# Order of TensorE's work in a slot of a Mamba-2 mixer kernel: the state matmuls from the second place to the third

## What is computed

```python
h = rmsnorm(x) * norm_w
proj = einsum('bsd,od->bso', h, in_proj_w)     # gate 8192 | hidden 8192, B 1024, C 1024 | dt 128
hBC = silu(causal_conv(hBC, conv_w, conv_b))   # 4 taps
hid, B, C = split(hBC)                         # 128 heads of 64; 8 groups of B and C, 128 states each
dt = softplus(dt + dt_bias); A = -exp(A_log) * dt
# chunked scan, in effect: y[i] = sum_{j<=i} (C_i . B_j) exp(cs_i - cs_j) dt_j hid_j
y = (Y_diag + Y_off) + Dp * hid
yg = y * silu(gate)
y = yg * rsqrt(mean over the group's 1024 channels of yg^2 + eps) * gnorm_w
out = x + einsum('bsd,od->bso', y, out_proj_w)
```

## Time and profile before

| what | value |
|---|---|
| median of 3 runs | 846.28 us (846.05 to 847.78) |
| profiled execution: its time, and its span | 846.1 us, 844.4 us |
| mean granted TensorE clock | 0.984 |
| TensorE matmuls busy | 792.3 us (94%) |
| TensorE weight loads busy | 611.8 us (72%) |
| VectorE, ScalarE, POOL busy | 626.7 us (74%), 599.9 us (71%), 633.9 us (75%) |
| DMA | 94.93 MB, mean 112 GB/s |

### The profile page before, as it was taken

One profiled execution on the slowest core, in us unless ns is written; L12 is line 12 of the kernel. 1 busy time (PEld: TensorE's weight loads), 2 busy tenths in 40 slices (PEclk: granted clock), 3 DMA queues, 4 the chain that ended last, 5 costly groups with the idle time before them and its releaser, 6 DMA issues.

```text
span 844.4 us, 13293 instructions
## 1 busy us (share of the span) xinstructions
PE 792.3 (94%) x4313; PEld 611.8 (72%) x4316; DVE 626.7 (74%) x757; ACT 599.9 (71%) x1046; POOL 633.9 (75%) x568
## 2 busy tenths in 40 slices
PE   4788899999999999999999999999999999989686
PEld 3566677777777777777777778777777777767563
DVE  5858878868686876776786867787677778697773
ACT  2487777888778876888688877887788857875341
POOL 5497975789767986789578985798678967893450
PEclk9899999999999999999999999999999999999996
DMA  8253232433253324334233415333342424420001
GB/s 278 67 186 122 90 125 89 126 126 125 68 181 125 118 94 150 125 113 136 87 125 125 125 62 165 124 113 121 129 128 98 153 88 141 125 88 1 5 2 50
DMA packets 48812, 94.93 MB, mean 112 GB/s; under 512 B 3952, under 2 KB 36848, under 8 KB 48784
## 3 DMA queue, kind: packets, MB, share of 16 engines
q1 hardware_dynamic: 48784, 94.58, 34.2%
HBM read 93.26 MB, written 1.31 MB: 112 GB/s over the span
## 4 chain that ended last, share of the span: by engine, by line
PE 59%; DVE 19%; ACT 10%; issue 9%; POOL 1%; POOLq 1%; ACTq 0%; DVEq 0%
PE ps_z L1071 19%; PE ps_out L1177 15%; PE ps_h L1071 12%; PE ps_y L1164 7%; DVE conv_bc L729 4%; ACT decay L539 3%; DVE conv L729 3%; PE ps_t L1049 2%; DVE decay L787 2%; ACT L539 2%; ACT conv L487 2%; DVE v L842 2%; DVE yg L848 1%; ACT conv_bc L471 1%; DVE y_lo L854 1%
## 5 line engine op out<-in xcount | busy, mean ns | idle before, releaser
L729 DVE SCALAR_TENSOR_TENSOR conv<-ps_h,w_raw,conv 128x510 f32<-128x510 f32 (+2 forms) x192 | 143.3, 746 | 100.7 <-ACT conv L487 96.0
L539 ACT ACTIVATE decay<-csx,cs_own 128x256 f32<-128x256 f32 (+1 forms) x512 | 184.4, 443 | 1.2 <-POOL csx L342 0.2
L304 POOL TENSOR_TENSOR win_lo<-w_raw,win_hi 128x1024 fp32r<-128x1024 f32 x64 | 152.8, 2387 | 0.7 <-DMA csx<-cs_rows 0.7
L399 POOL TENSOR_TENSOR sqacc<-sqacc,sq 128x512 f32<-128x512 f32 x47 | 70.5, 1500 | 106.9 <-ACT sq L575 106.9
L787 DVE TENSOR_TENSOR decay<-decay,cbm 128x1536 f32<-128x1536 f32 x64 | 127.9, 1998 | 2.8 <-ACT decay L539 2.8
L547 ACT ACTIVATE hidT<-conv 128x512 f32<-128x512 f32 x64 | 40.5, 633 | 100.5 <-DVE conv L729 100.5
L1164 PE MATMUL ps_y<-decay,hid_dt 128*64 128x256 f32 (+1 forms) x1024 | 98.5, 335 | 13.7 <-DVE hid_dt L831 13.7
L1164 PEld LDWEIGHTS ps_y<-decay,hid_dt 128*64 128x64 f32 x1024 | 64.0, 137 | 56.4 <-DVE hid_dt L831 19.5
L342 POOL TENSOR_SCALAR_AFFINE_SELECT csx<-csx 128x512 f32<-128x512 f32 x128 | 104.1, 838 | 0.0
L1177 PE MATMUL ps_out<-wout_hi,y_lo 128*128 128x512 f32 x256 | 101.5, 396 | 0.0
L1177 PE MATMUL ps_out<-wout_hi,y_hi 128*128 128x512 f32 x256 | 101.1, 395 | 0.0
(11 more groups left out here) (300 smaller groups left out, 1500.3 us busy)
## 6 DMA issues: line engine op xcount, KB each, us to landing
w_raw<-in_wmain SPq DMA_DIRECT2D x64, 772.0 KB, 4.3
csx<-cs_rows SPq DMA_DIRECT2D x128, 256.0 KB, 3.5
bc_raw<-in_wbc SPq DMA_DIRECT2D x8, 517.0 KB, 3.5
ctx_raw<-in_ctx SPq DMA_DIRECT2D x1, 2048.0 KB, 12.8
acc<-in_x SPq DMA_DIRECT2D x4, 256.0 KB, 3.4
bc_raw<-in_wffn SPq DMA_DIRECT2D x2, 512.0 KB, 4.1
out_x<-acc SPq DMA_DIRECT2D x4, 256.0 KB, 2.2
csx<-in_wdt SPq DMA_DIRECT2D x1, 256.0 KB, 5.0
```

Of the source, the lines that this page charges most:

```text
L304: eng.tensor_tensor(win_lo[:, r2, :], w_raw[:, r4, 0:W_IN], win_hi[:, r2, :].bitcast(f32), ALU.subtract).then_inc(low_win, 1)
L399: eng.tensor_tensor(sqacc[:], sqacc[:], sq[:, (k - 1) % 2, :], ALU.add).then_inc(pool_sq, 1)
L539: done = eng.activation(decay[:, r2, b, h, lo:lo + n], csx[:, r2, b, h, lo:lo + n], ACT.Exp, bias=cs_own[:, r2, t, h:h + 1])
L729: eng.scalar_tensor_tensor(out=out_b[:, :, back:], in0=src_b[:, :, 0:S - back], scalar=w[:, TAPS - 1 - back:TAPS - back], in1=out_b[:, :, ...
```

## The change

In slots with k from 1 to 7, the state matmuls stand behind the gate projection instead of ahead of it; in slot 1 the channel sums move along with them. In slot 0 of groups 1 to 7 the order is as before, and in slot 0 of the first group there is nothing to move. No instruction is added or left out, and every wait stays with its instruction.

```diff
@@ slot() of the TensorE block @@
                 project(ps_h[:], win_hi[:, r2, 0:KT * P], win_lo[:, r2, 0:KT * P], pe_hid)
                 if first and k == 0:
                     start_up()
-                if not (first and k == 0):
+                if k == 0 and not first:
                     scan_heads(s, k)
                 if k == 0:
...
-                if k == 1 and not first:
-                    sum_channels(g - 1)
 
                 if not (first and k == 0):
                     eng.wait_ge(act_gate, s)
...
                     if k == PPG - 1 and not last:
                         eng.wait_ge(dve_convbc, 6 * (g + 1) + 3)
                     project(ps_z[:], win_hi[:, r2, KT * P:], win_lo[:, r2, KT * P:], pe_gate)
+                if k > 0:
+                    scan_heads(s, k)
+                if k == 1 and not first:
+                    sum_channels(g - 1)
                 if not (first and k < 2):
                     project_out(s, g, k)
```

## The result

The changed kernel takes 857.46 us (median, 856.3 to 857.57, 4 runs) against 846.72 us before (846.05 to 847.78, 4 runs): a ratio of 1.0112, 95% interval 1.0081 to 1.0143. It is slower, and 857.46 lies inside the stated range of 849.5 to 859.5, some 3 us above the forecast of 854.7. The profiled execution took 857.42 us, its span is 855.7 us, 11.3 more than the span of before.

What follows compares the result with a forecast made beforehand. TensorE was taken to set the pace of plain slots, a ScalarE and VectorE loop close behind. Middle groups +10.6, first group -1.5, last -0.5 sum to +8.6 on 846.1: 854.7 us, range 849.5 to 859.5.

Steps and rivals of the forecast that it cites:

- TensorE's own work: nothing: Plain slots: moving the ps_y block costs TensorE nothing; slots stay 10.45 us, holes of 0.36 and 0.17 move along.
- Slot 7, 1.85: Slot 7: ps_z's wait for the next B convolution is uncovered; loss 1.85 us (1.6 to 2.3), floor 0.79.
- P: Start of ps_z in slot 7, counted from the slot's start: 3.59 at the floor, about 4.75 with late decays.
- Slot 5, -0.38: Slot 5 of the six middle groups: the wait for hid_dt goes, 0.74 less the block's 0.36, winning 0.38 us.
- The way to L471: Later scan, y_hi and POOL's selects in slots 5 and 6 delay the decays, so slot 7's tap L471 starts later.
- The loop's 10.12: Plain slots: ScalarE and VectorE form a second loop of 10.12 us against TensorE's 10.45, slack 0.33 a slot.
- First group, -1.5: First group: ps_z fills the hid_dt waits in slots 3 and 5; 1.5 us kept of some 8 (0.5 to 3).
- Last group and tail, -0.5: Last group: no B columns to wait for, but the tail scan still waits for hid_dt; -0.5 us (-0.7 to +0.3).
- A: Rival: TensorE's hid_dt waits vanish and nothing replaces them, 832.3 us, or milder about 845; chance of faster 0.06.
- B: Rival: slot 7 pays only the floor because the decays do not move; 848.4 down to 847 us; chance 0.07.
- C, the clock: Rival: holes of near 2 us in seven slots drop TensorE's clock to half; 862 us; chance 0.07.
- The rule on the port: Slot 6: VectorE's later yg could fall behind POOL's selects, up to 0.7 us a group; rows alone say 0.1.

Runs made afterwards that it cites:

- experiment 4: New order in slots 1 and 2 alone, against the kernel before: 854.76 us, ratio 1.0087.
- experiments 1: New order in slots 1 to 6, slot 7 in the old order, against the kernel before: 850.22 us, ratio 1.0037.
- experiment 2: New order in slot 7 alone, old order in all other slots, against the kernel before: 855.47 us, ratio 1.0097.
- kernel 8: Full change with POOL's selects ahead of the weight splits except in the first group, and slot 6's square cut to 8 of 512 columns: 867.8 us, ratio 1.0243.
- kernel 7: Full change with POOL's selects on csx ahead of the weight splits, except in the first group: 870.34 us, ratio 1.0254 to the kernel before.
- experiment 6: Full change with ScalarE's square in slot 6 cut to 8 of 512 columns: 858.0 us, ratio 1.0116 to the kernel before.
- kernels 9: Kernel before, old TensorE order, with POOL's selects ahead of the weight splits except in the first group: 852.8 us, ratio 1.0053.
- 11: Full change with the first group kept in the old order: 856.91 us, ratio 1.0108 to the kernel before.
- Experiment 10: Full change with 40 small matmuls ahead of the state matmuls in slot 5 of the first group: 863.02 us, ratio 1.0189 to the kernel before.
- 12: Kernel before, old order, with POOL making the upper B and C weights in slot 3 instead of slot 4: 852.76 us, ratio 1.0052.
- experiment 3: New order in slots 1 to 4 alone, against the kernel before: 869.27 us, ratio 1.0261.

## Why the prediction was right

*TensorE's own work: nothing.* Right: 10.45 us a plain slot, the two holes unchanged and moved with the block; experiment 4 shows it for two slots by themselves.

*Slot 7, 1.85.* Measured 15.07 - 13.22 = 1.85. The split into a floor (0.79) and a lateness (the rest) is what experiments 1 and 2 measure: the floor is 0.69, the lateness brings the rest, and 8 against 7 shows L471 passing on one for one. That the figure is right to the hundredth is luck. The prediction's own path gave P about 4.75, a loss of 1.95, and 1.85 was taken from no row; P is 4.77, and the stretch behind it 10.30 instead of 10.42, here and in experiment 2, which takes the 0.1 off again.

*Slot 0, 0.3.* Measured 0.36. *Slot 5, -0.38.* Right, only the block's own 0.36 is left in groups 1 to 6. Together 1.77 forecast, 1.79 measured: +10.75 against +10.6.

*The way to L471.* y_hi at 9.2 in slot 6 was forecast, from which L471 follows some 1.6 into slot 7; it is 9.32 and 1.61. The reason given in the prediction, POOL's selects in slots 5 and 6, is shown for slot 6 by experiment 6. One part of the way was not foreseen. In slot 4 VectorE's yg, which starts 1.1 later than before, takes 1.61 instead of 0.72:

```profile
375.31 1.61 DVE L848 TENSOR_TENSOR yg<-v,gate 128x512 f32<-128x512 f32 x1
```

With it y_hi stands at T+9.88 in slot 4, 9.57 in slot 5 and 9.32 in slot 6: a lateness of 1.9 of which the loop sheds 0.3 a slot, and not a steady 0.9 up to slot 4, as forecast. How much of L471's 1.61 comes by slot 4 and how much by the selects, no run separates. In experiment 4 the loop shed only 0.1 a slot, with a yg of 1.10. The loop's 10.12 itself has one term misread: "yg to y_hi 0.78" is the duration of yg; from start to start have 1.01, because there y_hi stands behind the gate. In the changed kernel, where yg is the later one, it is 0.73 (364.86 to 365.59), so the slack of 0.33 stands for undisturbed slots.

*First group, -1.5.* This is the term that failed. The mark at its end is 1.2 us later, so the term is 2.7 off, all of the difference between forecast and profile. The mark holds two things. The first 0.79 is there before slot 3: its tap L487 starts at 74.12 instead of 73.33 (before, then after), and kernels 9 and 11, whose first group has the old order, have it at 73.95 and 74.61. So this part can't be put down to the new order.

```profile
73.33 0.76 ACT L487 ACTIVATE conv<-ps_h,w_raw 128x512 f32<-128x512 f32 x1
```

```profile
74.12 0.76 ACT L487 ACTIVATE conv<-ps_h,w_raw 128x512 f32<-128x512 f32 x1
```

From that tap to L471 of slot 7 it is 120.01 - 73.33 = 46.68 before (46.68 and 46.69 in kernels 9 and 11) and 120.11 - 74.12 = 45.99 after (45.96 in kernel 7): 0.7 won, where the forecast had 2.6. From L471 to the mark the new order costs 1.1 (18.17 before, 19.27 after), as forecast. So the order costs the first group 0.4 us from slot 3 on, and the step that failed is "1.70 at 102.78, about 1.5 in slot 3 ... I make it 2.6 at L471".

The 1.5 of slot 3 came: counted from the tap, yg of slot 4 starts 1.43 earlier. The 1.70 of slot 5 didn't. The gate came 1.9 earlier there, at 100.90, but y_hi stands where it was, at 103.33 against 103.27, because it now waits for yg, and yg for the scan; and the scan's wait for hid_dt, which ps_z was to fill, is still there. TensorE comes to slot 7 1.4 us earlier (117.44 against 118.85) and not some 4. The lines after, weight loads and then ScalarE:

```profile
98.16 0.29 PEld L1166 LDWEIGHTS ps_y<-decay,hid_dt 128*64 128x64 f32 x4 [3.72 <-DVE hid_dt L831]
...
103.33 0.73 ACT L569 ACTIVATE y_hi<-yg,w_raw 128x512 fp32r<-128x512 f32 x1 [1.86 <-DVE yg L848]
```

In slot 4 part of the lead was lost too. VectorE's y_lo, before and then after:

```profile
94.30 1.78 DVE L854 SCALAR_TENSOR_TENSOR y_lo<-yg,w_raw,y_hi 128x512 fp32r<-128x512 f32 x1
```

```profile
91.88 2.89 DVE L854 SCALAR_TENSOR_TENSOR y_lo<-yg,w_raw,y_hi 128x512 fp32r<-128x512 f32 x1
```

y_lo starts 2.42 us earlier, mostly because the decay product ahead of it takes 2.59 instead of 3.96. Then it takes 2.89 instead of 1.78, beside POOL's split of the B and C weights (`wbc_lo`, 3.78 instead of 2.71), and the first operation on the context tile 1.49 instead of 0.41. From the start of yg to the end of hid_dt VectorE needs 9.39 instead of 8.83; hid_dt ends at 98.11 against 98.19. Experiment 10 shows that TensorE's half clock there is of little account; that the contention on VectorE cost the 0.56 is read from the durations and was not tested by itself.

*Last group and tail, -0.5.* Measured -0.6 from the last B·C products to the end, by luck. The last scan came 86.04 us behind the mark against 85.91, and its wait for hid_dt grew from 1.02 to 2.70; nothing was won there. The 0.8 was gained behind it, where nothing was changed and where kernels 9, 11 and 12 took 66.7, 65.9 and 66.5 us against 67.5 before and 66.7 after.

*The rivals.* A is out: the waits for hid_dt shrank by 7.1 us, not 13.8, and the wait for conv_bc alone grew by 12.1. B's floor is real (experiment 2), but its condition didn't hold, as the decays did move. Experiment 2 costs 1.0% and not B's 0.2% because it has neither the 0.38 of slot 5 nor the 2.0 us that B counted for the first and last groups. C, the clock, did not happen in the changed kernel's slot 7: groups 2 to 6 are all 93.9 behind holes of 2.0, and in the first group the clock stood at 1.00 behind the 3.14 too. It happened in experiments 3, 7 and 8 behind holes of 2.97, some 3.2 and 2.76 us, in some groups and not in others. The Trainium skill, "TensorE: Matmul & The Clock Gate", section "HAM oscillation — how this bites in real kernels", tells of a wait in each tile after which the next one starts cold; slot 7 of the changed kernel, with its 2.0 us, doesn't show that, slot 5 of experiment 3 shows it in part of the groups.

*The rule on the port.* Rows: the changed kernel's yg of slot 6 takes 0.87, as before, so the 0.7 a group weighed in the prediction didn't come there. In slot 4 yg does lengthen, to the 1.61 shown above, beside POOL's split of the B and C weights. In kernel 7, where yg starts beside win_lo, it takes 2.05, and in the first group y_lo lengthens as shown above. The Trainium skill, "SBUF — State Buffer", section "Who interferes with whom", has an exclusive lock between the two engines; these rows agree. The loss weighed for slot 6 came in slot 4, with another partner.

## What to carry to other kernels

When work on the engine that sets the pace is moved later, ask which banks the work it changes places with must wait for: the block that moved back was the cover of a wait that no list of waits showed, because it had a microsecond of slack. An engine chain with nearly the same period as the bound one sheds a delay slowly, 0.1 to 0.3 us a slot here; compare the two periods, and take the second from slots where its operations are disturbed too. A wait at the bound engine is worth only what the engines behind it can use. And before a term is read from one pair of profiles, see how far its mark moves between kernels that are alike up to there.

## What the runs showed of the hardware

The pace of VectorE and POOL depends on which operation starts beside which: the same yg took 0.69, 0.87, 1.10, 1.61 and 2.05 us, the same two selects 1.22 and 3.20 us, by where their partners stood. In experiment 3 one such meeting, in five of the six middle groups and not in the sixth, was worth 1.15 us of TensorE's wait. Behind holes of 2.76 us (kernel 8), 2.97 (kernel 3) and some 3.2 (kernel 7) in TensorE's weight loads the granted clock fell, to 0.50 where it was read behind the hole, in three or four of the middle groups and stayed up in others of the same execution. In slot 7 of the first group it fell behind 2.56 (kernel 6) and stayed at 1.00 behind 3.14 (the changed kernel). Behind the six holes of 2.0 of the changed kernel it stayed. Behind a fall a slot took 1.4 to 2.7 us more.
